# Inverse deviations by GpSimd powers, and the W1 and gate weight work one operation a slot later

## The reference

```python
x = x + conv_attention(ln_c(x))   # 1x1 q, k, v of 8 heads; softmax in windows of 8x8; 3x3 convolution of v added; 1x1 output
t = to_tokens(x)
t = t + ffn(ln_t(t))              # 8 experts, the best two for each token
```

```python
def ln(v, eps):                   # eps 1e-6 ahead of the attention, 1e-5 ahead of the experts
    m = mean(v, -1); s = var(v, -1)
    return (v - m) / sqrt(s + eps)

def ffn(x):
    gate = x @ Wg + bg
    top_w, top_i = top_k(gate, 2); w = softmax(top_w)
    return sum(w[e] * (gelu(x @ W1[e] + b1[e]) @ W2[e] + b2[e]) for e in top_i)
```

## Time and profile before

| | |
|---|---|
| three runs | 445.94 us median (444.67 to 448.31) |
| profiled execution | 446.38 us |
| its span from first to last instruction | 444.6 us |
| busy: PE, DVE, POOL, ACT | 381.1, 356.1, 306.4, 284.8 us |

### The profile page before, as it was taken

How to read it: one execution, slowest core, us unless ns; L and a number is a source line. 1 busy time by engine, 2 the same in 40 slices (tenths; PEclk the granted TensorE clock), 3 DMA queues, 4 the chain that set the end, 5 groups by cost and what they waited for, 6 DMA issues and landing times.

```text
span 444.6 us, 15399 instructions
## 1 busy us (share of the span) xinstructions
PE 381.1 (86%) x5543; PEld 241.7 (54%) x5543; DVE 356.1 (80%) x1214; ACT 284.8 (64%) x609; POOL 306.4 (69%) x392
## 2 busy tenths in 40 slices
PE   8897988989999979979979878887888988888950
PEld 8344434444555535534444434343778887877950
DVE  4678979987798998898898979896587898888630
ACT  2565786699788778778778566417556655556630
POOL 4233447675755788797887785875777777777776
PEclk9999989999999999999999989969899999999995
DMA  9915900000000000000000010112433323233300
GB/s 213 245 48 156 249 3 0 1 1 2 2 0 4 7 20 20 13 20 20 14 26 20 8 37 20 39 43 75 101 88 85 80 68 68 63 85 77 79 27 0
DMA packets 35396, 23.65 MB, mean 53 GB/s; under 512 B 13633, under 2 KB 32816, under 8 KB 35065
## 3 DMA queue, kind: packets, MB, share of 16 engines
q1 hardware_dynamic: 29480, 15.75, 15.0%
q0 software_dynamic: 4960, 6.45, 4.6%
q10 hardware_dynamic: 880, 0.48, 0.7%
HBM read 14.11 MB, written 9.27 MB: 53 GB/s over the span
## 4 chain that ended last, share of the span: by engine, by line
PE 36%; DVE 29%; issue 13%; ACT 9%; POOL 7%; DVEq 2%; DMA 2%; ACTq 0%; POOLq 0%
PE bank L1500 8%; PE bank L1421 6%; PE bank L1542 3%; DVE bt L1315 3%; PE bank L1518 3%; DVE mx L1193 3%; POOL out L674 3%; PE bank L1529 3%; PE bank L1696 2%; DVE rowb L1170 2%; PE bank L1679 2%; DVE bt L1318 2%; POOL pn L657 2%; DVE topi L992 2%; DVEq L445 2%
## 5 line engine op out<-in xcount | busy, mean ns | idle before, releaser
L657 POOL TENSOR_TENSOR pn<-pe_,rs 128x512 f32<-128x512 f32 x64 | 67.2, 1050 | 69.7 <-DVE rs L1204 65.6
L899 ACT ACTIVATE aa<-bank 128x512 f32<-128x512 f32 x91 | 54.4, 598 | 47.9 <-PE bank L1679 46.9
L633 POOL DMA_INDIRECT rows_hbm<-rowb,posu x64 | 65.5, 1023 | 22.5 <-issue 15.4
L1500 PE MATMUL bank<-aa,bd 64*64 64x256 f32 x512 | 70.1, 390 | 12.4 <-ACT pt L825 8.9
L674 POOL DMA_INDIRECT out<-bt,zs x63 | 62.3, 989 | 19.2 <-issue 14.9
L1503 PE MATMUL bank<-pt,bt 64*64 64x256 f32 x512 | 70.1, 391 | 0.0
L1193 DVE TENSOR_REDUCE mx<-bank 128x8 f32<-128x512 f32 x64 | 43.9, 685 | 24.6 <-PE bank L1500 24.3
L837 ACT ACTIVATE pe_<-sc 128x512 f32<-128x512 f32 x64 | 40.6, 635 | 35.5 <-DVE sc L1196 28.4
L1500 PEld LDWEIGHTS bank<-aa,bd 64*64 64x64 f32 x512 | 33.3, 132 | 46.4 <-issue 34.6
L797 ACT COPY zs<-bank 128x512 f32<-128x512 f32 x64 | 37.2, 582 | 16.5 <-PE bank L1503 16.5
L1518 PE MATMUL bank<-xsp,cv 128*128 128x512 f16 x144 | 42.3, 403 | 5.0 <-ACT ys L859 2.7
(11 more groups left out here) (290 smaller groups left out, 906.9 us busy)
## 6 DMA issues: line engine op xcount, KB each, us to landing
zs<-rows_hbm SPq DMA_DIRECT2D x91, 66.0 KB, 1.9
wloc<-in_L_conv_w_local SPq DMA_DIRECT2D x2, 1152.0 KB, 9.2
rows_hbm<-zrow SPq DMA_DIRECT2D x1, 1914.0 KB, 14.2
x_sb<-in_x SPq DMA_DIRECT2D x3, 512.0 KB, 10.8
wloc<-in_w SPq DMA_DIRECT2D x1, 1024.0 KB, 5.8
wloc<-in_w_last SPq DMA_DIRECT2D x1, 1024.0 KB, 8.5
rows_hbm<-rowb,posu POOLq DMA_INDIRECT x64
out<-bt,zs POOLq DMA_INDIRECT x63, 2.2
```

Of the source, the lines that this page charges most:

```text
L633: nc.gpsimd.indirect_dma_start(out=rows_hbm, out_offset=bass.IndirectOffsetOnAxis(ap=posu[:, t:t + 1], axis=0), in_=rowb[:, t], in_offset= ...
L657: nc.gpsimd.tensor_tensor(pn[:, v % 2, :].rearrange("p (h j) -> p h j", h=HEADS), pe_[:, v % 2], rs[:, v % 2].unsqueeze(2).broadcast_to([P ...
L899: nc.scalar.activation(hh[:, j % 2], hidb[j % 2][:].rearrange("p (q n) -> p q n", q=4), ACT.Gelu, scale=1.0 / (XS * WS)).then_inc(gelu_rea ...
L1500: scored = nc.tensor.matmul(dots[v % 2][same, w * 2 * P:(w + 1) * 2 * P], xq[same, t % 2, 2 * v + w], aa[same, t % 2, :, j0:j0 + WT], star ...
```

## The change

For the last 48 tiles the square root on ACT goes. Six powers on POOL (first_powers, eight tiles each, ahead of the normalisation in slots (2, 0) to (3, 1)) write rstd = variance ** -0.5 directly, and DVE makes the same Newton step in two parts: tiles 16 to 23 in (2, 1), the other 40 in (4, 0) (refine). The last operation of refine isn't waited for on DVE itself. POOL waits for the second part ahead of the normalisation of group 6. fold_last goes from group 2 to 3, the high halves of W1 from group 3 to 4, the low halves from group 3 to 5. The gate weight operations go from the start of group 3 into the four slots of group 4, one in each (the memset with the first), after the sum and reciprocal of the slot.

```diff
@@ POOL
+                    if is_step(g, 6):
+                        pool.wait_ge(rstd_ready, 4)
...
+            def first_powers(g, u):
+
+                k = 4 * g + u - 8
+                if k < 0 or QT + k * BT >= NT:
+                    return
+                cols_k = slice(QT + k * BT, QT + (k + 1) * BT)
+                if k == 0:
+                    pool.wait_ge(sq_in, 3)
+                    pool.wait_ge(rows_set, 1)
+                nc.gpsimd.tensor_tensor(rstd[:, cols_k], vc[:, cols_k], half_pow[:], ALU.pow).then_inc(first_power, 1)
...
                     for b, k in due("send", g, u):
                         send(b, k)
+                    first_powers(g, u)
...
-                    if is_step(g, 2):
+                    if is_step(g, 3):
                         fold_last(u)
@@ ACT
-                    if is_step(g, 2) and u == 1:
-
-                        act.wait_ge(sq_in, 3)
-                        nc.scalar.sqrt(vb[:, QT:], va[:, QT:]).then_inc(sq_done, 1)
-                    if is_step(g, 3):
+                    if is_step(g, 4):
 
                         act.wait_ge(w1_folded, u + 1)
@@ DVE
+            def refine(count, lo, hi):
+
+                r, a, b_, v = (t[:, lo:hi] for t in (rstd, va, vb, vc))
+                dve.wait_ge(first_power, (hi - QT) // BT)
+                link(nc.vector.tensor_tensor(b_, r, r, ALU.mult))
+                link(nc.vector.tensor_tensor(a, b_, v, ALU.mult))
+                link(nc.vector.tensor_scalar(a, a, -0.5 * XS, 1.5 * XS, ALU.mult, ALU.add))
+                nc.vector.tensor_tensor(r, r, a, ALU.mult).then_inc(rstd_ready, 1)
...
+            def gate_weights(u):
+
+                if u == 0:
+                    dve.wait_ge(ffn_in, 16 * 3)
+                    nc.vector.tensor_tensor(wg_sb[:], wg_sb[:], wgl_sb[:], ALU.subtract).then_inc(gatew_step, 1)
+                    nc.vector.memset(oh[:, BT], 0.0).then_inc(gatew_ready, 1)
+                dve.wait_ge(gatew_step, max(u, 1))
+                if u == 1:
+                    nc.vector.tensor_scalar(wg_sb[:], wg_sb[:], WS, None, ALU.mult).then_inc(gatew_step, 1)
+                if u == 2:
+                    nc.vector.tensor_copy(wg_hl[:, 0], wg_sb[:]).then_inc(gatew_step, 1)
+                if u == 3:
+                    nc.vector.tensor_tensor(wg_hl[:, 1], wg_sb[:], wg_hl[:, 0], ALU.subtract).then_inc(gatew_ready, 1)
...
-                if is_step(g, 3):
-
-                    dve.wait_ge(ffn_in, 16 * 3)
-                    link(nc.vector.tensor_tensor(wg_sb[:], wg_sb[:], wgl_sb[:], ALU.subtract))
-                    link(nc.vector.tensor_scalar(wg_sb[:], wg_sb[:], WS, None, ALU.mult))
-                    link(nc.vector.tensor_copy(wg_hl[:, 0], wg_sb[:]))
-                    nc.vector.tensor_tensor(wg_hl[:, 1], wg_sb[:], wg_hl[:, 0], ALU.subtract).then_inc(gatew_ready, 1)
-                    nc.vector.memset(oh[:, BT], 0.0).then_inc(gatew_ready, 1)
...
-                    if is_step(g, 3):
+                    if is_step(g, 4):
+                        gate_weights(u)
+                    if is_step(g, 5):
 
                         dve.wait_ge(w1_high, u + 1)
...
-                    if is_step(g, 2) and u == 2:
-                        rsqrt(3, QT, NT)
+                    if is_step(g, 2) and u == 1:
+                        refine(3, QT, QT + BT)
+                    if is_step(g, 4) and u == 0:
+                        refine(4, QT + BT, NT)
```

More of the change, by code:

```diff
@@ L325, in program @@
         gatew_ready = sem("gatew_ready")
+        gatew_step = sem("gatew_step")
         dve_step = sem("dve_step")
@@ L332, in program @@
         sq_done = sem("sq_done")
+        first_power = sem("first_power")
         zeroed = sem("zeroed")
```

## The result

The changed kernel takes 444.2 us (median of 20 runs, 442.97 to 447.08), the kernel before 447.04 beside it (20 runs). The ratio is **0.9949, 95% interval 0.993 to 0.9967**: 2.3 us won by the means of the runs (2.8 by their medians), where 4.6 were forecast. Applied to the 445.94 us of the runs that the forecast started from, that is 443.7. It lies inside the range of 438.9 to 445.2 and above the forecast's own 439.9 to 443.0. The profiled execution takes 445.42 us with a span of 443.6.

The account below looks back on a forecast made before the run. The prediction took the chain of waits, nearly all PE in a quiet group, as the bound. 6.37 - 0.65 - 0.8 - 0.3 = 4.62 us won from 445.94 gave 441.3 us, 8-in-10 range 438.9 to 445.2.

Parts of the forecast that it names:

- The ceiling of 6.37: From slot 2 of group 2 to group 5's start: 42.57 us against 36.20 at quiet pace, the most the change can win.
- Square root out, refine in (2,1): Group 2: table loads and half-speed stretch go, from a 3.68 us excess; refine delays the maximum, giving back 0.65 us.
- POOL's lag and ACT's products in group 4: POOL leaves group 3 3.8 us late and ACT gets W1 products: together 0.8 us given back, bounds 0 and 6.5.
- W1's low halves: Group 5: DVE gets 4.4 to 5.8 us more work, of which 0.3 us on the path; bounds 0 and 2.0.
- Rival 1: POOL bounds group 3 at stretched fold prices (1.72 instead of 1.27 us); 2.55 us of lag comes through: 443.5 us, chance 0.12.
- the sign given: Profile sign that the forecast is right: POOL without idle time ahead of pn from slot (2,1) to (4,1).
- Rival 3, the lock: Group 2: the first refine waits for the power behind pn; about 2.5 us less won, 443.8 us, chance 0.06.
- Rival 2: The excess only moves: new waits in groups 3 to 5 eat the 4.6 us; 445.9 us, chance 0.10.
- Rival 4: Loop of pn, exponential, sum, reciprocal puts all 10.0 us of powers on the path: 449.6 or 451.3 us, chance 0.05.
- The marks: PE's expected slot starts if right: (2,3) near 61 us, (3,0) near 64, (4,0) near 78, (5,0) near 94.

Follow-up runs that it names:

- the moves alone: Changed kernel with the square root back on ACT; only folds, gate weights and W1 moved: ratio 0.9953 to the kernel before.
- the kernel before with 8 and with 16 waits: Kernel before plus 8 or 16 already met waits on POOL (four or eight instructions) ahead of its first normalisation: ratios 1.0005 and 1.0056.
- the best kernel: Changed kernel with 18 already met waits on POOL and b2's low half moved from slot (5,3) to (5,0): ratio 0.9907 to the kernel before.
- powers-alone kernel: Changed kernel with folds, gate weights and W1 back where the kernel before has them: ratio 1.0091; with 18 met waits on POOL added, 1.0012.
- the kernels with 18 and 36 waits: Changed kernel plus already met waits on POOL: with 18, ratio 0.9914 and 0.9924 repeated; with 36, 0.9916.
- b2 early: Changed kernel with b2's low half on DVE moved from slot (5,3) to (5,0): ratio 0.9961 without added waits, 0.9907 with 18.

## Why the prediction came out short

**The step that failed** is "A shift at (6,0) should pass to the end, since all later steps follow one another and no transfer at a fixed time holds them." Up to (6,0) the sum held. After it 2.7 us were lost: 1.96 in group 8 to the stop, 0.34 in group 9 at a lower clock (0.50 from 158.8 to 162.2 us, 0.90 over its window; PE had just stood 2.69 us), 0.41 in group 6 to b2's low half. What held the later steps in group 8 is no transfer at a fixed time, but a stop that goes with the count of POOL's instructions (there with 199 ahead of the scatter, in five kernels of five, and in none of the nine others). The prediction costed what was added to POOL in microseconds only, and asked nowhere what eight more instructions do to the place of everything behind them.

**The ceiling of 6.37** was partly chance. "PE's idle stretch of 2.2 us shrinks below 1; I take it that the half-speed stretch goes with it": all four kernels with the square root on ACT have both table loads and nearly the same idle stretch. PE's clock falls to 0.51 behind it in two (the kernel before from 61.0 us, the moves alone from 61.6: PE waits 1.95 and 1.96 us for bt, group 2 takes 17.93 and 17.94) and stays at 1.00 in two (the kernel before with 8 and with 16 waits: 2.12 and 2.22 us, 16.89 and 16.99). The window of the kernel before with 16 waits:

```profile
52.00:65.00 13.00, 9.96 (x86) 5.14 (x87) 11.54 (x32) 10.79 (x18) 4.89 (x5) 1.00 0.15 31
```

About 1.0 us of the excess was so the clock of that one execution. The win by (6,0) is 4.1 to 5.4 us, by which of the kernels before one compares; the forecast's 4.62 lies between, and the best kernel's 0.9907 is 4.1. The excess was also read a little off: 64.42, 110.34 and 113.10 are pieces of the chain 0.07 us behind the first matmul of their slot; by first matmuls a quiet group takes 14.34 and the excess is 6.58.

**Square root out, refine in (2,1)**: right for refine, by luck for the root. From (2,2) to (3,0) take 7.91 us, 0.53 over the quiet 7.38 of the prediction; 0.65 was left for it. The last table load of the stage is at 17.70 us. What the powers add to the moves in group 2 is 17.94 (moves alone) - 14.94 = 3.00, against 3.68 - 0.65 = 3.03. But about 1.0 of it is the half-clock stretch of the moves alone; against the 16.89 and 16.99 without such a stretch some 2.0 are left.

**POOL's lag and ACT's products in group 4**: right, 0.8 forecast. Group 4 is 0.67 over 14.41; the moves alone, without the powers' lag, are 0.37 over, which is the 0.4 of ACT, and the other 0.3 I put down to the lag. Group 3 gave back nothing (14.21).

**W1's low halves**: 0.3 forecast in group 5, 0.41 measured at the start of group 6. DVE's b2 step, 0.68 us before, took 1.41 beside a pn, right in front of the maximum of (6,0). That pn runs from 110.45 to 111.83, and the b2 step stands on the chain of waits. From the timeline of DVE after:

```profile
110.96 1.41 DVE L1281 TENSOR_TENSOR wrec<-wloc,wrec 32x512 f16<-32x512 f32 x1
112.40 0.69 DVE L1220 TENSOR_REDUCE mx<-bank 128x8 f32<-128x512 f32 x1
```

**Rival 1** has its sign without its price. POOL has no idle time ahead of pn from 67.11 on (it had 0.48 us at 59.46 and 0.69 at 63.36, against the sign given), and an exponential waits for pn. From the timeline of POOL and ACT after:

```profile
67.11 1.04 POOL L673 TENSOR_TENSOR pn<-pe_,rs 128x512 f32<-128x512 f32 x1
...
68.23 0.63 ACT L853 ACTIVATE pe_<-sc 128x512 f32<-128x512 f32 x1 [0.44 <-POOL pn L673]
...
94.76 1.04 POOL L673 TENSOR_TENSOR pn<-pe_,rs 128x512 f32<-128x512 f32 x1 [0.42 <-DVE rs L1231]
```

The next idle time ahead of pn is 0.42 us at 94.76. One exponential waited 0.44 us for pn, and another, at 90.68, stood 0.57 us and started right behind the end of one; the folds kept to 1.27 us and the powers to 1.64 (single lines after the earlier trace rows):

```profile
L631 POOL TENSOR_TENSOR rstd<-vc,half_pow x6: 1635/1640/1676, 57.3 to 75.2; 128x8 f32<-128x8 f32 x6
...
L638 POOL TENSOR_TENSOR wloc<-wloc x4: 1267/1272/1275, 73.9 to 85.9; 128x512 f32<-128x512 f32 x4
...
L1276 DVE SCALAR_TENSOR_TENSOR wrec<-wloc,wrec x4: 641/812/1186, 98.1 to 110.3; 128x512 f16<-128x512 f32 x4
```

The chain of waits runs through POOL from 66 to 90 us, and costs 0.3 us: an engine that is on the chain because it has just caught up is not yet an engine that is late.

**Rival 3, the lock** (a power would hold up the first refine as the fold holds up the gate subtraction, 1.20 us in the earlier trace rows): wrong, as the prediction argued from the earlier trace rows. The first refine after, and POOL beside it, in the timeline:

```profile
59.46 1.04 POOL L673 TENSOR_TENSOR pn<-pe_,rs 128x512 f32<-128x512 f32 x1 [0.48 <-DVE rs L1231]
60.46 1.64 POOL L631 TENSOR_TENSOR rstd<-vc,half_pow 128x8 f32<-128x8 f32 x1
...
59.86 0.66 DVE L966 TENSOR_TENSOR vb<-rstd 128x8 f32<-128x8 f32 x1
60.56 0.17 DVE L967 TENSOR_TENSOR va<-vb,vc 128x8 f32<-128x8 f32 x1
...
60.96 0.17 DVE L969 TENSOR_TENSOR rstd<-rstd,va 128x8 f32<-128x8 f32 x1
```

The first step is stretched to the end of pn (0.66 us); the next three run in 0.17 each inside the power. The powers-alone kernel shows the other side: pn, xn and hl in a row held a DVE step for 2.90 us.

**The times of the rivals**: 443.7 stands right at those of rivals 1 and 3 (443.5 and 443.8). That is luck, since what they name cost 0.3 and nothing. Rival 2 (the win is eaten) has the right idea, but by a way that it doesn't name, and only about half is eaten. Rival 4's loop didn't close: group 2 to 4 are shorter, with all six powers in them.

**The marks**: less the 1.46 us of the late start, (2,3) came at 61.4, (3,0) at 64.0, (4,0) at 78.2 and (5,0) at 93.3, against 61, 64, 78 and 94.

**What stays open.** That the stop is a wait for POOL's own instructions is my reading of the count and of the transfer, behind which POOL's 199th instruction never starts sooner than 1.30 us in 14 traces. It isn't shown: no row names the engine that a transfer of q14 is for. Why the transfer starts at a count of 190 in one kernel and only at 198 in another, no run shows. And of the 4.9 to 5.4 us by which the kernels with 18 and 36 waits and that with b2 early are ahead at (15,0), the totals show 3.4 to 4.1: in most of them the rest after (15,0) takes 188.1 us instead of 186.1 in the kernel before. The clock there differs, 0.91 and 0.83 from 250 to 270 us. It goes so in all 14 traces: with 0.91 the rest takes 186.1 to 186.5 us, with 0.83 it takes 187.2 to 188.2. All five kernels with the stop have 0.91, but so have the kernel before and the changed one with 36 waits. The window of the kernel before:

```profile
250.00:270.00 20.00, 14.48 (x124) 7.49 (x121) 16.62 (x62) 10.49 (x20) 14.85 (x17) 0.91 0.09 28
```

The same window of the kernel with 18 waits and b2 early:

```profile
250.00:270.00 20.00, 14.48 (x118) 7.85 (x122) 15.56 (x45) 10.72 (x21) 12.27 (x13) 0.83 0.08 24
```

Whether this follows from the earlier start or is chance wasn't settled.

## What to carry to other kernels

When an edit adds instructions to an engine, look after its last group too: compare group lengths to the end, and look for idle time of "issue" with nothing recorded behind it. If one appears in code that wasn't touched, add a few met waits ahead of it before you look for a cause in the edit; the order of two versions can turn on it (b2 early stands at 0.9961 without and at 0.9907 with the waits). Move an engine's extra work and the work that it shares with a neighbour apart together: by (6,0) the powers without the moves won nothing or 2.2 us, by how POOL's and DVE's steps fell, the moves without powers 2.7, both together 5.4 (some 4.1 against a kernel before without the half-clock stretch).

## What the runs showed of the hardware

- POOL stood still for 2.3 to 2.6 us with nothing recorded but transfers of instructions, at a place that went with the count of its instructions (199 ahead of a scatter: five kernels of five; 191, 195, 202, 208, 217: none of nine). The 199th recorded instruction started no sooner than 1.30 us after the transfer had landed, in all 14 traces. In the changed kernel that was 148.92 to 149.40 for the transfer and 150.70 for the instruction.
- A power on GpSimd of 128x8 (1.64 us) didn't hold up DVE's refine steps with two SBUF inputs (0.17 us inside it in the changed kernel); pn alone stretched the first one (0.66 us), and pn, xn and hl in a row a low half of W1 (2.90 us in the powers alone, 0.64 in the shortest of the changed kernel). Which came first wasn't fixed: of two executions alike to 0.02 us until then, the step took 2.90 us in one and 0.76 in the other, where it came ahead of pn and pn took 1.49 instead of 1.05.
- PE's clock after nearly the same idle stretch, 1.95 to 2.22 us ahead of bt, fell in two of four kernels (0.51 from 61.0 to 64.4 us in the kernel before, 0.51 from 61.6 to 65.0 in the moves alone) and stayed at 1.00 in the other two, which are the kernel before with 8 and 16 empty waits.
